# Who issues the three small transfers of the row maxima in a four-layer attention and feed-forward kernel

## The chip, the cores and the metric

The kernel runs on one core of a Trainium2 chip. Its time is the device time of one execution in microseconds (us), inputs and outputs in device memory. Before the change the median of three runs is 6420.63 us, from 6415.23 to 6424.23.

## The reference

Sixteen sequences (B = 16) of 512 tokens of width 256 go through four residual layers, each after a layer norm. The second input is a context of 1601 tokens for each sequence.

```
x = x + attention0(norm(x), ctx)      # 16 heads of 16; q and k are layer-normed per head, scores times 4, softmax, then Wp
x = x + ffn0(norm(x))                 # 256 -> 64 -> 1024, gelu, -> 64 -> 256
x = x + attention1(norm(x), ctx)      # one head of 16, scores normalised over a row, softmax, head tiled 16 times, Wout
x = x + soft_moe(norm(x))             # logits with phi, softmax over the batch and over slots, 64 experts of 256 x 256
```

What matters here is layer 0: for each sequence and each of 16 heads a 512 x 1601 matrix of scores, its row maxima, its exponentials, and their product with the values.

## The kernel before, in words

The kernel has two stages. `stage_one` (to about 4400 us of the profile) computes the first three layers, `stage_two` the last one. The change is in `stage_one` alone.

**Groups and steps.** The 16 heads of a sequence ("image" `b`) are taken in G = 4 groups of HG = 4 heads. There are 64 groups in all, numbered n = 4b + g. The 1601 keys are cut into KC = 13 chunks, of which the last has 65 keys. One step is one key chunk of one group, so a group has 13 steps (c = 0 to 12) and an image has 52. In a step TensorE computes four transposed score tiles, one a head (`score_columns`, matmul at L832), ScalarE takes the exponential of each (`exponentials`, L1107, `probs`), and TensorE multiplies them with the values (`weigh_values`, L843).

**Row maxima.** The softmax needs each query's maximum. It is computed one group ahead: TensorE computes the scores of group n + 1 in 64 pieces (`row_piece`, L810), VectorE reduces them (L1271). In step c = 11 of group n the negated maxima are transposed, and VectorE splits them into three bf16 parts (`maxima_rows`, L1285 to L1289), 16 rows of 128 in the tile `nT`, and raises `nm_ready`. Three transfers of 4 KB then write the parts into rows 96 to 98 of the query stack `qst` of group n + 1 (`load_maxima`, L592, semaphore `nm_loaded`), so that the score matmul, which contracts over 99 rows, subtracts the maximum by itself. Hence the first score matmul of a group waits for the transfers:

```
if c == 0 and j == 0:
    pe.wait_ge(nm_loaded, 48 * (b * G + g + 1))
```

**What else is woven in.** All other work of stage one is cut into small operations. The table `WOVEN` gives each a place: a step and one of three places in it. Every engine walks through steps and places in the same order and does its own part of each operation. This work belongs to other images: the head of image b + 1 (projections, norms, the bf16 planes of its keys and queries) and the tail of image b - 1 (output projection, the two later layers).

**Queues.** In stage one every transfer is issued by SyncE, in the order of that walk: blocks of the context (`ld`, tile `cin`), planes and values stored and loaded again (`ldS`: twelve loads into `kst` and `qst` for one group; `ldV`: `vaug`), the tail's `xw` and `kv1T` (`ldX`), and its stores (`st3`). SyncE issues the maxima of group n + 1 at the start of step c = 12 of group n, ahead of that step's woven work. ScalarE issues no transfer in stage one; in stage two it issues the stores of `logit_scratch`, `y_scratch` and `out`.

Of the kernel before, what the change touches and what calls it, by code (L numbers as in the profile page):

```python
# [12 lines left out]
P = 128  # L13
B, S, D = 16, 512, 256
NK = 1601
QT = S // P
KC = -(-NK // P)
# [3 lines left out]
G = H // HG  # L21
# [17 lines left out]
def key_rows(c):  # L39
    return P if c < KC - 1 else KL  # L40
# [196 lines left out]
OUT_STEP, MAX_STEP = 2, KC - AHEAD  # L237
# [83 lines left out]
def stage_one(nc, x, ctx_d, mask, w, x3_d, xn_d, xnT_d, ident, psum):  # L321

    with ExitStack() as st:
# [48 lines left out]
        qst = [sb(f"qst{g}", [P, HG, S], BF16) for g in range(G)]  # L372
# [4 lines left out]
        nT = sb("nT", [HG * QT, 3, P], BF16)  # L377
# [52 lines left out]
        nm_ready = sem("nm_ready")  # L430
        nm_loaded = sem("nm_loaded")
# [25 lines left out]
        def woven_steps(it, steps, s, place):  # L457

            for of, label in WOVEN[s][place]:
                b = it + of  # L460
                if 0 <= b < B and label[0] in steps:
                    steps[label[0]](b, *label[1:])

        def alone(it, steps):
            for s in range(STEPS):
                for place in range(3):
                    woven_steps(it, steps, s, place)
# [4 lines left out]
        def _(sp):  # L472
# [113 lines left out]
                sp.wait_ge(t_act, at("t_act", b, "xT", 3, 1))  # L586
                sp.dma_start(xnT_d[b], xnT[:, :, :]).then_inc(x_stored, 16)

            def load_maxima(n):
                sp.wait_ge(nm_ready, n + 1)  # L590
                for r in range(3):
                    sp.dma_start(qst[n % G][96 + r:97 + r, :, :].rearrange("o j (t q) -> o (j t) q", q=P),  # L592
                                 nT[:, r, :]).then_inc(nm_loaded, 16)

            steps = {"ld": load_block, "stV": store_values, "stkv1": store_keys_one, "stX": store_planes,
                     "ldS": load_stacks, "ldV": load_values, "ldX": load_tail, "st3": store_tail}

# [1 line left out]
            sp.wait_ge(setup_pool, SETUP_POOL)  # L599
            alone(-2, steps)  # L600
            alone(-1, steps)
            load_maxima(0)
            for b in range(B):
                for s in range(STEPS):
                    n, c = b * G + s // KC, s % KC
                    if c == MAX_STEP + 1 and n + 1 < B * G:
                        load_maxima(n + 1)
                    for place in range(3):
                        woven_steps(b, steps, s, place)
            alone(B, steps)  # L610
# [433 lines left out]
        def _(act):  # L1044
# [57 lines left out]
            def exponentials(b, g, c, j):  # L1102
                m, k = key_rows(c), STEPS * b + KC * g + c
                act.wait_ge(s_full, 4 * k + j + 1)
                if j == 0 and k >= 2:
                    act.wait_ge(pv_mm, k - 1)
                fn(probs[0:m, 4 * (k % 2) + j, :], bank[S_BANK[j % 2]][0:m, :], ACT.Exp,  # L1107
                   scale=float(HD) ** 0.5).then_inc(s_exp, 1)

            def heads_copied(n):  # L1110
                act.wait_ge(pv_mm, KC * (n + 1))
                if n >= 1:
                    act.wait_ge(m_full, RING["out", n - 1] + 1)
                fn(o_sb[:, :], bank[V_BANK], ACT.Copy).then_inc(o_copied, 1)
# [49 lines left out]
                     "s1": layer_one_exp, "o1": layer_one_copied}  # L1164

            alone(-1, steps)
            for b in range(B):
                for s in range(STEPS):
                    g, c = s // KC, s % KC
                    n = b * G + g  # L1170
                    exponentials(b, g, c, 0)
                    if c == 1 and n >= 1:
                        heads_copied(n - 1)
                    woven_steps(b, steps, s, 0)
                    exponentials(b, g, c, 1)
                    woven_steps(b, steps, s, 1)
                    exponentials(b, g, c, 2)
                    woven_steps(b, steps, s, 2)
                    exponentials(b, g, c, 3)
            heads_copied(B * G - 1)  # L1180
            alone(B, steps)

# [705 lines left out]
```

## Time and profile before

| | before |
|---|---|
| median of three runs | 6420.63 us |
| profiled execution | 6438.05 us |
| its span, first to last instruction | 6436.0 us |
| TensorE busy | 5770.0 us, 90% |
| VectorE busy | 3625.0 us, 56% |
| ScalarE busy | 3263.2 us, 51% |
| GpSimd busy | 2413.9 us, 38% |
| mean granted clock of TensorE | 0.955 |

The profile is of one execution. In it PE is TensorE (PEld its weight loads), DVE VectorE, ACT ScalarE, POOL GpSimd, SP SyncE; a `q` behind the name (SPq, ACTq) marks what the engine's queue of instructions does itself, such as issuing a transfer. "L832" is line 832 of the kernel. A tile's name stands as `output<-inputs`. A busy TensorE is not TensorE at its peak, since matmuls are pipelined and their ends are modelled. The granted clock is the share of full speed, 2.4 GHz, that TensorE was given; 0.5 is 1.2 GHz. In the timelines times count from the first instruction; neighbouring instructions of one line are merged into one row with their count ("x3"), and a row that is the first of an answer may start with the first instruction that still ran in the window asked for.

### The profile page before, as it was taken

The page shows a single profiled execution, that of the slowest core. Times are in us where ns is not written, and L with a number is a line of the kernel's source. Part 1 is how long each engine was busy: PE and PEld are TensorE (multiplying, and loading weights), DVE is VectorE, ACT ScalarE, POOL GpSimd, SP SyncE. Part 2 cuts the span into 40 slices and gives each one's busy share as a digit, 9 for nine tenths or more (in the row PEclk, how much of TensorE's full clock was granted, in tenths as well). Part 3 has the DMA queues.
Part 4 walks back from the last instruction along what each step waited for, and adds up shares of the span by engine and source line. Part 5 has one row for each costly group of instructions (what it writes and reads, how often), then busy time and mean ns, then how long its engine had stood idle before and what let it go on. Part 6 is the DMA issues. An engine that isn't in the chain of part 4 may idle for free. (4 is left out here: it accounts for less than half of the span.)

```text
span 6436.0 us, 94456 instructions
## 1 busy us (share of the span) xinstructions
PE 5770.0 (90%) x36221; PEld 2996.8 (47%) x36221; DVE 3625.0 (56%) x7015; ACT 3263.2 (51%) x6257; POOL 2413.9 (38%) x2686
## 2 busy tenths in 40 slices
PE   3799999999999998999989999896599999998999
PEld 1223333333333332333323333232488888877888
DVE  3565656656666665665666656660466666652333
ACT  1366666666665666666666666663222222223331
POOL 3226356263462644626436355344122222220000
PEclk9799999999999999999999999997799999999999
DMA  2441432414324233242332432310366666666553
GB/s 57 86 86 50 78 70 63 85 51 77 70 68 83 54 77 66 70 82 60 68 67 71 79 68 65 64 23 16 135 220 214 213 215 210 208 219 243 205 196 118
DMA packets 436274, 683.75 MB, mean 106 GB/s; under 512 B 63376, under 2 KB 336928, under 8 KB 433520
## 3 DMA queue, kind: packets, MB, share of 16 engines
q1 hardware_dynamic: 326000, 568.64, 34.4%
q10 hardware_dynamic: 109824, 109.07, 5.0%
q8 instruction: 288, 4.72, 0.3%
q14 instruction: 162, 1.33, 0.1%
HBM read 458.39 MB, written 218.39 MB: 105 GB/s over the span
## 5 line engine op out<-in xcount | busy, mean ns | idle before, releaser
L1271 DVE TENSOR_REDUCE mx<-psum 128x1 f32<-128x401 f32 x4096 | 2166.8, 569 | 1570.2 <-PE psum L810 1565.1
L1107 ACT ACTIVATE probs<-psum 128x512 f32<-128x512 f32 (+1 forms) x3328 | 1894.1, 601 | 907.9 <-PE psum L832 900.9
L810 PE MATMUL psum<-kst,qst 96*128 96x401 bf16 x4096 | 1365.1, 348 | 86.0 <-DMA qst<-q_planes 35.9
L832 PE MATMUL psum<-qst,kst 99*128 99x512 bf16 (+1 forms) x3328 | 1302.1, 392 | 109.7 <-ACT probs L1107 58.7
L810 PEld LDWEIGHTS psum<-kst,qst 96*128 96x128 bf16 x4096 | 406.3, 99 | 1339.5 <-DVE mx L1271 900.5
L843 PE MATMUL psum<-probs,vaug 128*17 128x512 f32 x6656 | 903.0, 615 | 0.0
L1565 POOL TENSOR_TENSOR disp<-disp,rz 128x2048 f32<-128x2048 f32 x64 | 294.4, 4601 | 930.3 <-DVE rz L1795 930.3
L832 PEld LDWEIGHTS psum<-qst,kst 99*128 99x128 bf16 (+1 forms) x3328 | 335.0, 101 | 522.7 <-ACT probs L1107 262.9
L1584 PE MATMUL psum<-phi,xT 128*128 128x128 f32 x4096 | 514.3, 280 | 39.6 <-DMA xT<-xnT_scratch 33.6
L1599 PE MATMUL psum<-disp,xnb 128*128 128x128 f32 x4096 | 492.7, 279 | 52.9 <-DMA xnb<-xn_scratch 34.2
L1584 PEld LDWEIGHTS psum<-phi,xT 128*128 128x128 f32 x4096 | 482.6, 194 | 87.3 <-issue 80.9
L1599 PEld LDWEIGHTS psum<-disp,xnb 128*128 128x128 f32 x4096 | 476.7, 194 | 62.0 <-DMA xnb<-xn_scratch 36.2
L679 POOL TENSOR_SCALAR rs<-mv 128x4 f32<-128x4 f32 x48 | 11.2, 232 | 1176.9 <-DVE mv L1323 1175.7
L763 PE MATMUL psum<-wkv,cT 128*128 128x512 f32 (+1 forms) x832 | 410.5, 616 | 16.9 <-ACT sq L1074 7.4
L1828 DVE COPY disp<-psum 128x512 f32<-128x512 f32 x256 | 177.0, 692 | 368.2 <-PE psum L1641 368.1
L1653 PE MATMUL psum<-disp 128*128 128x256 f32 x1536 | 367.4, 381 | 5.2 <-DVE xnb L1845 2.5
L1674 ACT ACTIVATE disp<-psum 128x512 f32<-128x512 f32 x256 | 152.2, 597 | 432.1 <-PE psum L1584 432.0
L1700 ACT ACTIVATE xT<-xT,nm 128x512 f32<-128x512 f32 x256 | 181.0, 709 | 348.2 <-DMA xT<-logit_scratch 339.9
L1802 DVE TENSOR_TENSOR ysb<-psum,be 128x512 f32<-128x512 f32 x128 | 88.6, 692 | 461.0 <-PE psum L1614 450.4
L1706 ACT ACTIVATE slT<-psum 128x512 f32<-128x512 f32 x128 | 76.4, 597 | 435.9 <-PE psum L1599 435.9
L1653 PEld LDWEIGHTS psum<-disp 128*128 128x128 f32 x1536 | 276.4, 190 | 40.4 <-DVE xnb L1845 5.6
L1614 PE MATMUL psum<-we,slT 128*32 128x256 f32 x4096 | 247.7, 382 | 0.0
(198 smaller groups left out, 7467.5 us busy)
## 6 DMA issues: line engine op xcount, KB each, us to landing
xnb<-xn_scratch SPq DMA_DIRECT2D x256, 512.0 KB, 3.7
kst<-k_planes SPq DMA_DIRECT2D x384, 200.1 KB, 8.8
logit_scratch<-disp ACTq DMA_DIRECT2D x64, 1024.0 KB, 4.9
xT<-logit_scratch SPq DMA_DIRECT2D x32, 2048.0 KB, 7.9
k_planes<-pl SPq DMA_DIRECT2D x96, 384.0 KB, 3.2
y_scratch<-ysb ACTq DMA_DIRECT2D x128, 256.0 KB, 4.9
vaug<-v_scratch SPq DMA_DIRECT2D x64, 442.0 KB, 3.7
v_scratch<-vst SPq DMA_DIRECT2D x48, 544.0 KB, 3.1
```

What stands on the lines that cost most here:

```text
L763: last = mm(hb[0:m, :], cT[:, n % 2, k, a * P:a * P + m], wkv[:, k, :], start=(k == 0), stop=(k == 1))
L810: mm(to[:, 0:PW], qst[g][0:NP, j, t * P:(t + 1) * P], kst[g][0:NP, j, k0:k0 + PW], start=True, stop=True).then_inc(m_full, 1)
L832: mm(bank[S_BANK[n % 2]][0:m, :], kst[g][0:NR, j, c * P:c * P + m], qst[g][0:NR, j, :], start=True, stop=True).then_inc(s_full, 1)
L843: last = mm(bank[V_BANK][32 * j:32 * j + HV, :], vaug[0:m, g % 2, c, HV * j:HV * (j + 1)], probs[0:m, 4 * (k % 2) + j, :], start=(c == 0), ...
L1107: fn(probs[0:m, 4 * (k % 2) + j, :], bank[S_BANK[j % 2]][0:m, :], ACT.Exp, scale=float(HD) ** 0.5).then_inc(s_exp, 1)
L1271: v.tensor_reduce(mx[:, n % 2, u // 4, u % 4:u % 4 + 1], bank[HOMES[r][0]][:, 0:PW], AX.X, ALU.max).then_inc(m_free, 1)
L1565: pool.tensor_tensor(d, d, rz[:, n % 2, None, :].broadcast_to((P, B, SL)), ALU.mult).then_inc(normed, 1)
L1584: last = mm(bank[u % 4][:, a * SL:(a + 1) * SL], xT[:, 4 * q + a, k, t * P:(t + 1) * P], phi[:, k, s * SL:(s + 1) * SL], start=(k == 0), s ...
L1599: last = mm(bank[4 + n % 2][:, (2 * a + h) * SL:(2 * a + h + 1) * SL], xnb[:, a, t, h * P:(h + 1) * P], disp[:, (QT * s + t) % RING, b, :] ...
L1614: last = mm(bank[6 + n % 2][32 * j:32 * j + 32, a * D:(a + 1) * D], slT[:, n % 2, a, k, 32 * j:32 * j + 32], we[:, s % 2, j, k, :], start= ...
L1653: last = mm(bank[4 + t][:, a * D:(a + 1) * D], exT[n % 4][:, t * P:(t + 1) * P], ya[b % 4][:, e, :], start=(e == 0 and a == 0), stop=(e == ...
L1700: fn(d, d, ACT.Exp, bias=nm[:, t, b:b + 1], accum_out=sums[:, b % 4, t, h:h + 1]).then_inc(c_exp, 1)
```

## The change

The three transfers of `load_maxima` are taken out of SyncE's program and put into ScalarE's, one behind each of the exponentials 0, 1 and 2 of step c = 12, so ahead of that place's woven work. The first of them waits for `nm_ready`. For the first group of all, ScalarE issues the three together before the first step. What is transferred, the semaphores and every other place stay as they are.

```
--- before.py
+++ after.py
@@ -586,12 +586,6 @@
                 sp.wait_ge(t_act, at("t_act", b, "xT", 3, 1))
                 sp.dma_start(xnT_d[b], xnT[:, :, :]).then_inc(x_stored, 16)
 
-            def load_maxima(n):
-                sp.wait_ge(nm_ready, n + 1)
-                for r in range(3):
-                    sp.dma_start(qst[n % G][96 + r:97 + r, :, :].rearrange("o j (t q) -> o (j t) q", q=P),
-                                 nT[:, r, :]).then_inc(nm_loaded, 16)
-
             steps = {"ld": load_block, "stV": store_values, "stkv1": store_keys_one, "stX": store_planes,
                      "ldS": load_stacks, "ldV": load_values, "ldX": load_tail, "st3": store_tail}
 
@@ -599,12 +593,8 @@
             sp.wait_ge(setup_pool, SETUP_POOL)
             alone(-2, steps)
             alone(-1, steps)
-            load_maxima(0)
             for b in range(B):
                 for s in range(STEPS):
-                    n, c = b * G + s // KC, s % KC
-                    if c == MAX_STEP + 1 and n + 1 < B * G:
-                        load_maxima(n + 1)
                     for place in range(3):
                         woven_steps(b, steps, s, place)
             alone(B, steps)
@@ -1107,6 +1097,12 @@
                 fn(probs[0:m, 4 * (k % 2) + j, :], bank[S_BANK[j % 2]][0:m, :], ACT.Exp,
                    scale=float(HD) ** 0.5).then_inc(s_exp, 1)
 
+            def load_maxima(n, r):
+                if r == 0:
+                    act.wait_ge(nm_ready, n + 1)
+                act.dma_start(qst[n % G][96 + r:97 + r, :, :].rearrange("o j (t q) -> o (j t) q", q=P),
+                              nT[:, r, :]).then_inc(nm_loaded, 16)
+
             def heads_copied(n):
                 act.wait_ge(pv_mm, KC * (n + 1))
                 if n >= 1:
@@ -1164,17 +1160,27 @@
                      "s1": layer_one_exp, "o1": layer_one_copied}
 
             alone(-1, steps)
+            for r in range(3):
+                load_maxima(0, r)
             for b in range(B):
                 for s in range(STEPS):
                     g, c = s // KC, s % KC
                     n = b * G + g
+
+                    def maximum_row(r):
+                        if c == MAX_STEP + 1 and n + 1 < B * G:
+                            load_maxima(n + 1, r)
+
                     exponentials(b, g, c, 0)
+                    maximum_row(0)
                     if c == 1 and n >= 1:
                         heads_copied(n - 1)
                     woven_steps(b, steps, s, 0)
                     exponentials(b, g, c, 1)
+                    maximum_row(1)
                     woven_steps(b, steps, s, 1)
                     exponentials(b, g, c, 2)
+                    maximum_row(2)
                     woven_steps(b, steps, s, 2)
                     exponentials(b, g, c, 3)
             heads_copied(B * G - 1)
```

## Rows read from the trace of the kernel before

**Rows 1.** Waits by engine: us in all, times, longest; TensorE, 236 to 4400 us.

```profile
PE psum L832 <- DMA qst<-nT: 46.6, 12, 5.7
```

**Rows 2.** The view of the tile nT: issues, and landing times.

```profile
L592 SPq DMA_DIRECT2D qst<-nT x192: 502/589/1610, 241.4 to 4344.4; - x192
...
DMA to landing us min/median/max: 1.6/2.1/11.9
```

**Rows 3.** Timeline (start, length, what) of SyncE's queue at a third change.

```profile
3299.20 2.68 SPq L557 DMA_DIRECT2D kst<-k_planes  x6
...
3316.37 1.84 SPq L592 DMA_DIRECT2D qst<-nT  x3
3323.20 2.65 SPq L557 DMA_DIRECT2D kst<-k_planes  x6
```

**Rows 4.** Timeline of TensorE: among them the first and last of 12 waits.

```profile
417.95 0.61 PE L832 MATMUL psum<-qst,kst 99*128 99x512 bf16 x1 [5.68 <-DMA qst<-nT]
...
3322.78 0.38 PE L832 MATMUL psum<-qst,kst 99*65 99x512 bf16 x1
...
3329.59 0.61 PE L832 MATMUL psum<-qst,kst 99*128 99x512 bf16 x1 [5.16 <-DMA qst<-nT]
...
4124.74 0.61 PE L832 MATMUL psum<-qst,kst 99*128 99x512 bf16 x1 [4.43 <-DMA qst<-nT]
```

**Rows 5.** Windows: length, PE, PEld, DVE, ACT, POOL busy, PE clock, DMA, GB/s.

```profile
3329.00:3332.00 3.00, 2.41 (x6) 0.94 (x8) 1.15 (x2) 1.20 (x2) 0.00 (x0) 0.50 1.07 132
```

**Rows 6.** Timeline of SyncE's queue at an image change.

```profile
1260.92 1.77 SPq L592 DMA_DIRECT2D qst<-nT  x3
1263.05 0.39 SPq L572 DMA_DIRECT2D xw<-in_x  x1
...
1264.03 0.47 SPq L579 DMA_DIRECT2D kv1T<-kv_scratch  x1
```

**Rows 7.** Timelines of ScalarE and TensorE at that image change.

```profile
1263.93 1.08 ACT L1107 ACTIVATE probs<-psum 65x512 f32<-65x512 f32 x2
...
1265.47 0.38 PE L832 MATMUL psum<-qst,kst 99*128 99x512 bf16 x1
```

**Rows 8.** Timeline of ScalarE in stage two: issues of its own.

```profile
4707.02 2.31 ACTq L1712 DMA_DIRECT2D y_scratch<-ysb  x1
...
4733.57 0.60 ACT L1674 ACTIVATE disp<-psum 128x512 f32<-128x512 f32 x1 [1.19 <-PE psum L1584]
4733.58 0.37 ACTq L1712 DMA_DIRECT2D y_scratch<-ysb  x1
```

**Rows 9.** Timeline of ScalarE at a first and a second change.

```profile
1332.44 1.08 ACT L1107 ACTIVATE probs<-psum 65x512 f32<-65x512 f32 x2
...
1674.48 0.59 ACT L1107 ACTIVATE probs<-psum 65x512 f32<-65x512 f32 x1
```

**Rows 10.** Timeline of TensorE at the same two changes.

```profile
1335.02 0.38 PE L832 MATMUL psum<-qst,kst 99*128 99x512 bf16 x1
...
1677.81 0.38 PE L832 MATMUL psum<-qst,kst 99*128 99x512 bf16 x1
```

**Rows 11.** Timelines at third changes, without a wait and with one.

```profile
1736.59 2.24 ACT L1107 ACTIVATE probs<-psum 65x512 f32<-65x512 f32 x4
...
1737.33 0.38 PE L832 MATMUL psum<-qst,kst 99*128 99x512 bf16 x1
...
3323.53 1.07 ACT L1107 ACTIVATE probs<-psum 65x512 f32<-65x512 f32 x2
```

**Rows 12.** Transfers issued in 4729 to 4735, then in 4750 to 4757 us.

```profile
y_scratch<-ysb ACTq DMA_DIRECT2D x1, 256.0 KB, 2.9
...
y_scratch<-ysb ACTq DMA_DIRECT2D x1, 256.0 KB, 5.6
```

**Rows 13.** Timeline of SyncE's queue just before the second of those stretches.

```profile
4748.77 0.43 SPq L1494 DMA_DIRECT2D we<-in_L_ffn_W  x1
```

**Rows 14.** Transfers issued in 1264 to 1265 us: size, us to landing.

```profile
kv1T<-kv_scratch SPq DMA_DIRECT2D x1, 8.1 KB, 3.9
```

More of the change, by code:

```diff
@@ L587, in store_tail @@
                 sp.dma_start(xnT_d[b], xnT[:, :, :]).then_inc(x_stored, 16)
[L589 to L593, printed above, removed]
             steps = {"ld": load_block, "stV": store_values, "stkv1": store_keys_one, "stX": store_planes,
@@ L601, in _ @@
             alone(-1, steps)
-            load_maxima(0)
             for b in range(B):
                 for s in range(STEPS):
-                    n, c = b * G + s // KC, s % KC
-                    if c == MAX_STEP + 1 and n + 1 < B * G:
-                        load_maxima(n + 1)
                     for place in range(3):
@@ L1108, in exponentials, with load_maxima @@
                    scale=float(HD) ** 0.5).then_inc(s_exp, 1)
+            def load_maxima(n, r):
+                if r == 0:
+                    act.wait_ge(nm_ready, n + 1)
+                act.dma_start(qst[n % G][96 + r:97 + r, :, :].rearrange("o j (t q) -> o (j t) q", q=P),
+                              nT[:, r, :]).then_inc(nm_loaded, 16)
             def heads_copied(n):
@@ L1166, in _ @@
             alone(-1, steps)
+            for r in range(3):
+                load_maxima(0, r)
             for b in range(B):
@@ L1170, in _, with maximum_row @@
                     n = b * G + g
+                    def maximum_row(r):
+                        if c == MAX_STEP + 1 and n + 1 < B * G:
+                            load_maxima(n + 1, r)
                     exponentials(b, g, c, 0)
+                    maximum_row(0)
                     if c == 1 and n >= 1:
@@ L1175, in _ @@
                     exponentials(b, g, c, 1)
+                    maximum_row(1)
                     woven_steps(b, steps, s, 1)
                     exponentials(b, g, c, 2)
+                    maximum_row(2)
                     woven_steps(b, steps, s, 2)
```

## The prediction

> **What bounds the kernel now.** I read the page's busy shares first, then the waits of TensorE, the view of the tile `nT`, and last the timelines around the places where one group of heads gives way to the next. TensorE is busy for 90% of the span (the table above). It takes its instructions in the order written, so in the first stage (to about 4400 us) a wait of TensorE is time added to the end unless a later wait shrinks by it. One wait there belongs to this change: TensorE stands before the first score matmul of a group (L832) for the maxima rows, 12 times, 46.6 us together, 5.7 us the longest [rows 1]. The wait does not come from a late issue: SyncE issues the three transfers about when `nT` is ready, spending 0.59 us on each, but they land after 1.6 us at best, 2.1 us as the median and 11.9 us at worst [rows 2].
>
> The slow landings have one place. An image has four groups, so 64 groups have 63 changes between them. I call the change from group 0 to 1 "first", 1 to 2 "second", 2 to 3 "third", and into group 0 of the next image "image change". The timeline of TensorE has all 12 waits at third changes, from the one of image 0, ended at 417.95, to that of image 14, ended at 4124.74 [rows 4]. The one of image 11: SyncE has put the stacks of later groups into its queue from 3299.20 on; the maxima are issued at 3316.37 into the same queue, behind that backlog, and the score matmul starts at 3329.59 after 5.16 us of waiting [rows 3, 4]. Afterwards the matmul takes 0.61 us where one before took 0.38, and the granted clock of 3329 to 3332 is 0.50, which is 1.2 of 2.4 GHz, after TensorE had stood still [rows 4, 5]. So a long wait costs more than its length. I estimate 1.2 us more each (one stretch of some 3 us at half speed does half its work, less what TensorE would have waited anyway). Before: 46.6 + 12 x 1.2 = 61 us that the change can win at most.
>
> **The change, part by part.**
>
> *Removed from SyncE*: 192 issues of 0.59 us [rows 2] and its wait for `nm_ready`. Worth nothing: SyncE's next operations wait for their own data (at an image change `xw` goes out at 1263.05, after the maxima's issue is over [rows 6]), and no TensorE wait but the one above is for a late issue of SyncE's. Were it wrong, loads would go out up to 3 x 0.59 = 1.8 us earlier, which could add to the traffic that the maxima meet.
>
> *Added to ScalarE*: the same 192 issues. The wait for `nm_ready` is free: at the image change the maxima were ready when SyncE issued them at 1260.92, and the last key chunk's exponentials that ScalarE must first reach run around 1263 to 1264 [rows 6, 7]. What is queued behind it, the exponentials and all woven copies, therefore does not stand. The issue itself: ScalarE's issue of `y_scratch` starts 0.01 us after an activation of 0.60 us and takes 0.37 us, within it [rows 8], so an issue hides under the exponential ahead of it. For these small transfers I take SyncE's 0.59 us against exponentials spaced 0.5 to 0.6 us: 0 to 0.2 us of delay a group. The dear end is an issue of 2.31 us, right behind a 1 MB store on the same queue [rows 8]. I take nothing for the delay in itself and keep 1 us x 15 image changes in the range.
>
> *Moved in time*: this is the cost. Before, all three were out when `nT` was ready, some 4.5 us ahead of the score matmul at an image change (1260.92 against 1265.47 [rows 6, 7]). After, the third goes out no sooner than the third exponential of the last chunk has begun. How long that is before the score matmul, read off the timelines without a wait:
> - first change: 1332.44 starts a row of two exponentials, the second of them is ours, at 1332.9; matmul 1335.02: 2.1 us [rows 9, 10].
> - second change: 1674.48 against 1677.81: 3.3 us [rows 9, 10].
> - third change: 1736.59 against 1737.33: 0.7 us [rows 11].
> - image change: 1263.93 against 1265.47: 1.5 us [rows 7].
>
> A transfer alone lands in about 1.7 us (between the 1.6 and the 2.1 of rows 2). So first and second changes stay free, while third and image changes wait **always**: at least 1.0 us and 0.2 us.
>
> *Third changes (15 of 16 with loads about)*: the backlog of SyncE's queue is now in another queue than the maxima. From below: the transfer runs as if alone, 1.7 - 0.7 = 1.0 us. From above: it still goes behind everything, and in image 11 behind a `kst` load issued at 3323.20, just ahead of our 3323.55 [rows 3, 11]; then it lands about when it does now or a little later, near 4.4 us. Nearest to it is ScalarE's `y_scratch` under SyncE's loads: 2.9 us in a usual stretch, 5.6 us in a stretch ahead of which, at 4748.77, SyncE had issued a 1 MB load [rows 12, 13], so a tax of up to 2.7 us behind a big load, and here the loads just ahead are small (200 KB) and the big backlog was given out 13 us ago. I take a tax of 0.8 us: 1.8 us x 15 = 27, and 1.0 for the last image, together 28 us.
>
> *Image changes (15)*: about our third issue (1263.93 plus some 0.2, so 1264.1) SyncE has just issued `xw` of 512 KB at 1263.05 and the `kv1T` loads to 1264.03 [rows 6]. From below, alone: 1264.1 + 1.7 = 1265.8, 0.4 us late. From above: like the 8.1 KB `kv1T` transfer that goes out at 1264.03 behind the same loads and takes 3.9 us [rows 6, 14]: 1267.9, 2.5 us late. The y_scratch pair says that a load issued just before on the other queue does hold a transfer up; I take 2.2 us, x 15 = 33 us.
>
> *Aftermath of the waits*: 30 waits near or above 1 us instead of 12 long ones; shorter ones should slow the clock less often, so 0.8 us each, 24 us; first and second changes 2 us in all.
>
> Sum after: 28 + 33 + 24 + 2 = 87 us, against 61 us before: **26 us slower**. The profiled execution took 6438.05 us (span 6436.0), which makes 6464; it lies 17 us above the median of the runs, so on the median's scale 6420.6 + 26 = 6447 us.
>
> The Trainium skill has a rule that speaks about the same disputed point. Its page "DMA: Bandwidth & Descriptors", section "Queues, rings and completion order", says that each of the DMA engines takes turns between the queues by packets of typically 9 to 17 descriptors, so a small transfer on a second queue would wait for one packet at most, not for a backlog. The 5.6 us against 2.9 us of rows 12 does not look like that; by the rule the image change would be near its low end and the result the first rival's.
>
> **Rivals.**
>
> *Faster: the second queue passes everything.* If the maxima wait for no more than the few descriptors under way, third changes cost 1.4 x 15 + 1 = 22 us, image changes 0.6 x 15 = 9, aftermath 10, together 41 against 61: 20 us faster, 6401. The place is ScalarE's empty queue in the first stage, the price what is left of the landing after the third exponential; it decides if the tax at an image change stays under about 1 us. For it: nothing else is on that queue before 4400 us. Against: rows 12.
>
> *Even.* The taxes come out between, say 1.4 us at image changes and 1.6 at third ones: 21 + 25 + 18 = 64 against 61, within 13 us of 6421.
>
> *Much slower: the backlog holds the second queue too.* Third changes 4.4 x 15 = 66 us, image changes 2.5 x 15 = 38, aftermath 30 x 0.8 = 24: 128 against 61, 67 slower, 6488. It decides from the point where the maxima land with the `kst` load issued before them. For it: rows 12. Against: the backlog at a third change was issued long ago, in small pieces.
>
> That the change does nothing is excluded by the order written: the third issue stands behind an exponential that begins 0.7 us before the matmul.
>
> **How the numbers follow.** Forecast 0.45, faster rival 0.22, even 0.2, much slower 0.13. The forecast's own range is 6430 to 6465. A measurement of this kernel can tell about 0.2%, 13 us, from no change (its three runs span 9 us). Faster by more: 0.2; within: 0.26, with edges of the forecast and the faster rival; slower: 0.54. The range for 8 in 10 reaches 22 us down and 61 up: 6398 to 6482.
>
> **What would show it.** Right: the wait for `qst<-nT` appears some 30 times, of 1 to 3 us, none above 3.5; it is at every image change, where there was none, and at every third change; none at second changes; the landing of the transfers has a median near 2 us and a worst of 4 to 5 us; ScalarE's busy time is the same. Wrong: landings at image changes under 2.2 us (the tax is not there, the faster rival), or waits of 4 us and more at third changes (the backlog holds both queues), or a first change that waits, or exponentials that stand behind issues of over 1 us. If the waits come out as said and the time does not, the term for the clock is at fault.

## The result, and the profile after

| | before | after |
|---|---|---|
| median | 6422.43 us (4 runs) | 6533.5 us (4 runs, 6508.97 to 6544.69) |
| profiled execution / its span | 6438.05 / 6436.0 us | 6528.45 / 6526.7 us |
| ratio after to before | | 1.0166, 95% interval 1.0132 to 1.0200 |
| first score matmul of stage one to the last | 4149.5 us | 4237.7 us |
| waits of TensorE for the maxima | 47 us | 99 us |
| time lost to the lower clock in stage one | 124 us | 159 us |

The change makes the kernel 111 us slower on the medians, 90 us between the two profiled executions. Of these, 88 us lie in stage one. The last row sums (1 - granted clock) over the clock records between the first and the last score matmul: 3.4 us at half clock lose 1.7. The two sums grow by 52 and by 35 us, 87 together, so the 88 us are accounted for. The other 20 us between 111 and 90 are the place of the profiled executions among the runs: the one before lies 16 us above its median, the one after 5 us below.

The waits of TensorE in stage one of the kernel after (against [rows 1]), and the view of `nT` (against [rows 2]); `L822` is the score matmul's line now, `L1103` that of the transfers:

```profile
PE psum L822 <- DMA qst<-nT: 99.3, 44, 5.3
PE psum L867 <- POOL xn L672: 67.9, 30, 2.9
PE psum L822 <- ACT probs L1097: 55.1, 90, 1.8
```

```profile
L1103 ACTq DMA_DIRECT2D qst<-nT x192: 510/527/1336, 237.7 to 4435.0; - x192
...
DMA to landing us min/median/max: 1.6/2.4/7.5
```

12 waits have become 44 (the view leaves out waits of under 0.15 us). The worst landing has come down from 11.9 to 7.5 us, but only because the transfers start later. Summed by place, the waits are: third changes 40.6 us (15 and one of 0.1 us; before 47.0 with the last image's), image changes 52.0 us (15, before 0.1), second changes 6.2 us (1.7 in image 0, 0.1 to 0.5 in 13 others), the very first group 0.7.

The image change into image 4 (against [rows 6] and [rows 7]), on the timelines of SyncE's queue, of ScalarE and of TensorE:

```profile
1273.97 0.38 SPq L572 DMA_DIRECT2D xw<-in_x  x1
1274.45 0.59 SPq L577 DMA_DIRECT2D kv1T<-kv_scratch  x1
1275.08 0.70 SPq L579 DMA_DIRECT2D kv1T<-kv_scratch  x1
```

```profile
1273.78 0.59 ACT L1097 ACTIVATE probs<-psum 65x512 f32<-65x512 f32 x1 [0.88 <-PE psum L822]
1273.78 0.57 ACTq L1103 DMA_DIRECT2D qst<-nT  x1
1274.40 0.59 ACT L1097 ACTIVATE probs<-psum 65x512 f32<-65x512 f32 x1
1274.42 0.57 ACTq L1103 DMA_DIRECT2D qst<-nT  x1
1275.04 0.59 ACT L1097 ACTIVATE probs<-psum 65x512 f32<-65x512 f32 x1
1275.06 0.58 ACTq L1103 DMA_DIRECT2D qst<-nT  x1
```

```profile
1280.63 0.61 PE L822 MATMUL psum<-qst,kst 99*128 99x512 bf16 x1 [3.92 <-DMA qst<-nT]
```

The reader sees each issue start with an exponential and end under it: ScalarE as an issuer costs nothing to speak of. The first transfer goes out at 1273.78, 0.2 us ahead of `xw`; the other two go out behind it. What that does to their landings, of the three, and what the neighbours took (transfers issued in 1273 to 1277):

```profile
DMA to landing us min/median/max: 1.7/4.5/5.5
```

```profile
xw<-in_x SPq DMA_DIRECT2D x1, 512.0 KB, 4.7
...
qst<-nT ACTq DMA_DIRECT2D x3, 4.0 KB, 4.5
kv1T<-kv_scratch SPq DMA_DIRECT2D x2, 8.1 KB, 5.4
```

1.7 us for the one ahead, 4.5 and 5.5 us for those behind. The third, 4 KB out of ScalarE's empty queue, takes as long as the two 8.1 KB `kv1T` transfers of SyncE's (5.4 us is the middle of 4.8 and 6.0), which were given out behind the same load.

Third changes show the same more plainly, since the backlog there is old. ScalarE and TensorE at that of image 11, where the first transfer was issued at 3386.91:

```profile
3388.42 0.51 ACTq L1103 DMA_DIRECT2D qst<-nT  x1
...
3390.14 0.51 ACTq L1103 DMA_DIRECT2D qst<-nT  x1
3390.28 0.68 ACT L1151 ACTIVATE hx<-psum,maskb 128x512 f32<-128x512 f32 x1
3390.85 1.07 ACT L1097 ACTIVATE probs<-psum 65x512 f32<-65x512 f32 x2
```

```profile
3395.91 0.39 PE L822 MATMUL psum<-qst,kst 99*128 99x512 bf16 x1 [4.17 <-DMA qst<-nT]
```

The last row of ScalarE holds the exponentials 2 and 3. The third issue, written behind exponential 2, went out 0.71 us before that exponential began, while ScalarE was still at two woven activations; so it is at 14 of the 16 third changes (0.87 us at the last one, not at the first). The packets by queue, first in 3387 to 3391.4, then in 3391.4 to 3393.4 (q1 is SyncE's queue, q10 ScalarE's):

```profile
q1 hardware_dynamic: 469, 0.55, 106.8%
```

```profile
q1 hardware_dynamic: 189, 0.30, 106.7%
q10 hardware_dynamic: 90, 0.01, 8.8%
```

For 4.5 us after the first issue not one packet of ScalarE's queue moves, while the stacks that SyncE had given out ahead of the transfers (24 loads for two groups, issued from 3366.43 to 3377.7 here, as the ones from 3299.20 on in [rows 3]) are worked off; then 90 packets of it move within 2 us. The order is not strict: when the first of them moved, five of the 24 loads had still to land, and the last of these landed at 3394.84, between the second transfer (3394.61) and the third (3395.87). Over all third and image changes of the kernel after, 373 of 392 times a transfer of SyncE's that had been issued earlier and was still out landed before the one of the maxima, the other 19 times at most 0.9 us behind it; of 564 issued later, while one of the maxima was still out, 546 landed behind it.

The clock behind the image change, the windows 1281 to 1285 and 1285 to 1289 of the kernel after, where the kernel before had 1.00 at the same place (columns as in [rows 5]):

```profile
1281.00:1285.00 4.00, 4.00 (x17) 3.06 (x16) 1.95 (x5) 2.28 (x4) 0.20 (x1) 0.50 1.08 137
1285.00:1289.00 4.00, 4.00 (x15) 0.73 (x13) 1.25 (x3) 1.64 (x3) 4.00 (x1) 0.50 1.03 127
```

### The profile page after: what moved, and what is told of

It reads as the page before. It is cut to its first block and busy times, and to the rows that moved or that the text cites. A ratio compares the mean times of both kernels' runs of the same rounds, so it can differ in the third digit from the quotient of the medians.

```text
span 6526.7 us, 94456 instructions
## 1 busy us (share of the span) xinstructions
PE 5805.8 (89%) x36221; PEld 3010.5 (46%) x36221; DVE 3629.4 (56%) x7015; ACT 3268.7 (50%) x6257; POOL 2408.9 (37%) x2686
## 5 line engine op out<-in xcount | busy, mean ns | idle before, releaser
L822 PE MATMUL psum<-qst,kst 99*128 99x512 bf16 (+1 forms) x3328 | 1314.4, 395 | 160.8 <-DMA qst<-nT 99.3
L822 PEld LDWEIGHTS psum<-qst,kst 99*128 99x128 bf16 (+1 forms) x3328 | 336.6, 101 | 586.8 <-ACT probs L1097 267.0
```

What stands on the lines that cost most here:

```text
L822: mm(bank[S_BANK[n % 2]][0:m, :], kst[g][0:NR, j, c * P:c * P + m], qst[g][0:NR, j, :], start=True, stop=True).then_inc(s_full, 1)
```

## The experiments

All ratios are to the kernel before, measured on the same chip, with 95% intervals; 3 rounds each. "Waits" are those of TensorE for the maxima, "clock" the time lost as in the table above, both of the profiled execution. The kernel before was run again with each set of kernels, with medians of 6414.52 to 6423.13 us by chip; a ratio is to the one of its own set.

| kernel | median us | ratio | waits us | clock us |
|---|---|---|---|---|
| before | 6423.13 (25 runs) | | 47 | 124 |
| after | 6533.5 | 1.0166 [1.0132, 1.0200] | 99 | 159 |
| act_early | 6427.61 | 0.9997 [0.9984, 1.0010] | 42 | 120 |
| sp_late | 6426.47 | 1.0005 [0.9992, 1.0018] | 47 | 108 |
| tail_after | 6454.85 | 1.0043 [1.0028, 1.0057] | 48 | 101 |
| stack_later | 6348.82 | 0.9881 [0.9863, 0.9898] | 0 | 75 |
| xw_rows | 6531.43 | 1.0172 [1.0148, 1.0197] | 88 | 147 |
| filled | 6536.83 | 1.0194 [1.0165, 1.0223] | 70 | 148 |
| stack_after | 6527.1 | 1.0167 [1.0132, 1.0201] | 94 | 147 |
| before_filled | 6407.94 | 0.9978 [0.9963, 0.9994] | 32 | 87 |
| paced | 6554.76 | 1.0208 [1.0181, 1.0235] | 93 | 165 |
| stack_paced | 6652.21 | 1.0366 [1.0346, 1.0387] | 187 | 236 |
| sp_behind | 6544.77 | 1.0200 [1.0168, 1.0233] | 129 | 188 |
| filled_long | 6487.34 | 1.0127 [1.0098, 1.0155] | 30 | 85 |

**act_early: the issuer alone.** From the changed kernel, `maximum_row` taking the step as well; each `+` names the call that now stands behind that exponential:

```
 exponentials(b, g, c, 0);  + maximum_row(MAX_STEP + 1, 2)      # maximum_row(at_c, r): if c == at_c
 exponentials(b, g, c, 2);  + maximum_row(MAX_STEP, 0)
 exponentials(b, g, c, 3);  + maximum_row(MAX_STEP, 1)
```

> The changed kernel, but ScalarE issues the three transfers as soon as the maxima are ready: behind exponentials 2 and 3 of step 11 and exponential 0 of step 12, about when SyncE issued them before. Theory A (what costs is the late issue, by which the transfers fall behind the loads that SyncE issues around an image change; queue and issuing engine matter little, and a transfer keeps its turn behind everything issued earlier on either queue): no waits for the maxima at image changes and second changes, third changes wait as in the kernel before (2 to 5 us each, 40 to 50 us in all), time 6410 to 6440 us. Theory B (ScalarE as issuer costs by itself, by blocking its queue): time stays above 6480 us. Theory C (a queue of its own lets the transfers pass the backlog if they are out early): third changes wait under 1 us each, time 6360 to 6390 us.

The time is that of the kernel before. ScalarE as issuer costs nothing measurable (B falls), and a queue of its own gives nothing (C falls): early out on the empty queue, the transfers still took up to 10.5 us at third changes.

```profile
PE psum L822 <- DMA qst<-nT: 42.1, 15, 6.0
```

**sp_late: the lateness alone.** From the kernel before:

```
+ sp.wait_ge(s_full, 4 * (KC * n - 1) + r + 1)      # before issue r, at place r of step 12
```

> The kernel before, with SyncE as issuer, but each of the three issues waits until the score tile of exponential 0, 1 and 2 of step 12 is there, so they go out as late as in the changed kernel, yet in SyncE's own order, ahead of the loads of the next image change. Theory A (being late costs by what it falls behind; no queue is special): image changes wait 0.2 to 0.6 us each, third changes 2 to 5 us as in the changed kernel, the sum of waits 50 to 60 us, time 6420 to 6450 us. Theory D (being late by itself costs what was seen, loads ahead or not): image changes wait about 3.4 us each, time 6500 us or more.

The same late issues on SyncE's queue, where `xw` comes behind them by the order written, cost nothing measurable. Image changes wait 0.20 us in most images (5.4 us in all), third changes 42 us. So lateness is not the price; what is let in front is. (The sum of the waits, 47 us, is a little under the 50 to 60 expected.)

**sp_behind: one queue, loads in front.** sp_late, with the loads of `xw` and `kv1T` moved between the first and the second transfer:

```
-    put(0.0, -1, "ldX")
+    put(51.0, 0, "ldX")
```

> sp_late (SyncE issues everything, the maxima late), but the loads of xw and kv1T of the image change are issued between the first and the second maxima transfer, about where they fall in time in the changed kernel. Theory A (both queues are served in the order of issue, so whose queue it is makes no difference): image changes wait 3 to 4.5 us each and the time is 6490 to 6560 us. Theory K (a second queue makes it worse than one: the transfers lose their turn to the other queue): waits of 1.5 to 2.5 us on one queue, the time at most 6475 us.

With everything in one queue the loss of the change is back, and the time is in theory A's range (K falls). The image change of image 4 waits 5.23 us:

```profile
1288.53 0.61 PE L835 MATMUL psum<-qst,kst 99*128 99x512 bf16 x1 [5.23 <-DMA qst<-nT]
```

The waits are longer than theory A said (88 us over 15 image changes, 5.9 each), because the second and third issue also queue behind five issues of 0.5 us on SyncE: the third goes out 1.3 us after TensorE began to wait, where it went out 1.6 us ahead of that in the kernel after. The landings themselves are no longer: the third took 4.5 us in the mean of the 15 image changes, against 5.0 in the kernel after.

**tail_after: two queues, loads held back.** From the changed kernel:

```
 sp.wait_ge(x_stored, at("x_stored", b - 1, "st3"))
+if b + 1 < B:
+    sp.wait_ge(nm_loaded, 48 * (G * (b + 1) + 1))
 sp.dma_start(xw...)
```

> The changed kernel, but at an image change SyncE holds back the loads of xw and kv1T until the three transfers have landed. Theory A (the wait at image changes comes from these loads, issued on the other queue just ahead of the second and third transfer): the wait there falls from 3.4 to 0.2 to 0.7 us each, the landing of the third transfer from 5.2 to about 2 us, time falls by 60 to 90 us to 6440 to 6470 us. Theory E (ScalarE's queue itself is slow to land what it issues back to back): the waits stay near 3 us and the time above 6500 us.

The waits at image changes fall from 52.0 us to 4.3, most of them 0.10 us each; at the one around 1263 us all three land in 1.7 us:

```profile
DMA to landing us min/median/max: 1.7/1.7/1.7
```

79 us of the 111 come back by this one wait of SyncE, and what remains is within 32 us of the kernel before. E falls. (Its runs spread from 6423 to 6462 us, and the profiled one is the lowest of ten, so the sums in the table flatter it.)

**paced: SyncE held back as before, but not issuing.** From the changed kernel, at the start of step 12:

```
+ sp.wait_ge(nm_ready, n + 2)
```

> The changed kernel, but SyncE still waits for nm_ready at the start of step 12, as it did when it issued the maxima, and issues nothing there. Theory A: nothing is queued behind that point that matters (the loads of the image change and of the third change come at the same times), so waits and time stay as in the changed kernel, 6515 to 6545 us. Rival J (part of the loss is that SyncE is no longer held back and its loads crowd the transfers): time falls by 20 us or more.

No gain (J falls); the time is 10 us above the range of theory A, and the ratio if anything a little above that of the kernel after (the intervals overlap).

**xw_rows: as many bytes, a quarter of the pieces.** From the changed kernel:

```
-sp.dma_start(xw[:, :, :], x[b].rearrange("(t p) d -> p t d", p=P))
+sp.dma_start(xw[:, :, :], x[b].rearrange("(p t) d -> p t d", p=P))
```

> The changed kernel, but the load of xw at an image change (512 KB) is read in 128 pieces of 4 KB instead of 512 pieces of 1 KB; the same bytes, other token order, so what the layers behind it compute is another permutation of the tokens. Theory A1 (the transfers wait for the bytes ahead of them to pass): waits at image changes stay at 3 to 3.5 us, time 6515 to 6540 us. Theory A2 (they wait for the pieces ahead to be made and taken one by one): the wait falls by 0.7 to 1.5 us each, time by 15 to 45 us.

This kernel is for its time alone: its tokens come into `xw` in another order than what is added to them, so its output is another. In the trace the load moves in 128 packets of 4 KB. Waits at image changes go from 3.5 to 3.1 us, the time stays (A1): the number of pieces of this load is not what the transfers wait for, in the main.

**stack_later: the backlog out of the way of the kernel before.**

```
-    put(head["X", 4, 0] + 2.2, 1, "ldS", 1)
+    put(39.2, 1, "ldS", 1)
```

> The kernel before, with one edit of the table: the twelve loads of group 1's stacks of the next image move from step 33.7 to 39.2, behind the third change. Theory A (the waits of the kernel before at third changes come from the backlog of these loads alone): the 12 waits vanish (under 5 us in all), landings of the maxima are at most 3 us, and with less time at half clock the kernel takes 6360 to 6385 us, faster than both. Rival F (the backlog moves with the loads and something else waits: the values, the context block or the first scores of the next image's groups): a new wait of similar size, time within 0.3% of 6422 us.

The waits are gone: in the waits of TensorE no row names `nT` any more, and the view of the tile has

```profile
DMA to landing us min/median/max: 1.6/1.7/3.6
```

It is 1.19% faster than the kernel before and the best of all. At 6348.8 it lies 11 us below A's range, so the gain was larger than expected: in the profile the lower clock costs 75 us in place of 124, so 50 us less. What share of the miss that is, no run tells. F falls.

**stack_after and stack_paced: the same edit on the changed kernel.** stack_after is the `put` above on the kernel after; stack_paced adds the wait of paced.

> The changed kernel with the loads of group 1's stacks moved behind the third change (as in stack_later), to see what the change costs where no backlog is. Theory A: third changes wait 0.9 to 1.3 us each (only the late issue), image changes 3 to 3.5 us each as before, first changes none; sum of waits 65 to 75 us and with the clock the kernel is 75 to 105 us slower than stack_later, 6425 to 6455 us. Rival (with the backlog gone the second queue is free and the loads of the image change no longer matter): within 30 us of stack_later, under 6380 us.

> stack_after with the same wait of SyncE for nm_ready kept, so that the moved loads of group 1's stacks can't run ahead of the third change. Theory A: third changes wait 0.9 to 1.4 us each (16 us in all, only the late issue), image changes 3 to 3.6 us each (50 us), second changes 0.3 to 0.5; with the clock 85 to 125 us slower than stack_later, 6435 to 6475 us. Rival (the second queue is taxed by any traffic): third changes stay above 2.5 us and the time above 6500 us.

Both expectations missed. In stack_after the waits at third changes remained at 38 us. SyncE's timeline shows why: the loads of group 1's stacks (the second pair of rows) went out at once behind those of group 0, ahead of the transfers (from 1212.31 on), although the table puts them behind the third change.

```profile
1192.27 2.68 SPq L557 DMA_DIRECT2D kst<-k_planes  x6
1194.99 2.77 SPq L559 DMA_DIRECT2D qst<-q_planes  x6
1197.81 2.77 SPq L557 DMA_DIRECT2D kst<-k_planes  x6
1200.62 2.77 SPq L559 DMA_DIRECT2D qst<-q_planes  x6
```

SyncE runs ahead of the steps as far as its waits let it. What held it at the third change in stack_later was its own wait for `nm_ready`, which the change had moved to ScalarE. With that wait back (stack_paced) it issues the twelve loads the moment the maxima are ready, at 1231.36, while ScalarE issues them from 1234.58 to 1237.81, and TensorE waits longest of all:

```profile
1231.36 2.65 SPq L557 DMA_DIRECT2D kst<-k_planes  x6
1234.05 2.78 SPq L559 DMA_DIRECT2D qst<-q_planes  x6
```

```profile
1248.59 0.61 PE L825 MATMUL psum<-qst,kst 99*128 99x512 bf16 x1 [9.17 <-DMA qst<-nT]
```

So with the change's issue on ScalarE the kernel with this line moved is 2.8% (stack_after, 6527.1) and 4.8% (stack_paced, 6652.2) slower than without it (6348.8). That is again the order of issue over both queues, here at its dearest.

**filled, before_filled, filled_long: is it the clock?** Extra score matmuls into a bank that is overwritten next, ahead of the wait:

```
+for _ in range(k):      # filled: k = 6 at groups 0 and 3; before_filled: 6 at group 3; filled_long: 16 at group 0, 12 at group 3
+    mm(bank[S_BANK[0]][0:m, :], kst[g][0:NP, 0, 0:m], qst[g][0:NP, 0, :], start=True, stop=True)
 pe.wait_ge(nm_loaded, ...)
```

The wait for the exponentials stands ahead of them now.

> The changed kernel, but at image changes and third changes TensorE runs six extra score matmuls of 0.38 us (into the bank that the next one overwrites) before it waits for the maxima, so it is busy for 2.3 us of a wait of about 3. Theory G (a third of the loss is the half clock after TensorE stood still): the waits shrink by what the fillers take, the time at half clock in the first stage falls from 159 us lost to 100 to 130 us lost, and the time falls to 6480 to 6510 us though no transfer lands earlier. Rival H (the half clock has nothing to do with these waits): lost time by the clock stays near 159 us, time 6530 us or a little above.

> The kernel before with six extra score matmuls ahead of the wait at third changes only. Theory G: the waits shrink from 47 us to about 20 us and the time lost by the clock from 124 to 90 to 110 us; time 6390 to 6415 us. Rival H: time 6423 us or up to 10 us above, since three of the third changes had no wait to fill.

> The changed kernel with 16 extra score matmuls (3.4 us at 0.21 us each) ahead of the wait at an image change and 12 (2.6 us) at a third change, so TensorE hardly stands still in these waits. Theory G (half clock follows standing still): time lost by the clock in the first stage falls from 159 to 90 to 115 us, the waits from 99 to 40 us or less, the time to 6475 to 6510 us. Rival H (the half clock does not follow these waits): lost time by the clock stays above 140 us, time 6530 us or above.

filled settles nothing: in a row the matmuls take 0.21 us each, not the 0.38 that I had reckoned with, so six covered 1.3 us of waits of 3; clock and time hardly moved, and its expectation missed. before_filled gained 0.22% [0.06, 0.37] with 37 us less lost to the clock, though 32 us of waits were left where 20 were expected. filled_long covers the waits. Landings are no earlier, yet the kernel is 46 us faster than the kernel after (6487 against 6533, and 46 us between the profiled executions too), with the clock's loss at 85 us instead of 159. But each was measured against a set of runs of the kernel before of its own; by these ratios, 1.0127 and 1.0166, the gain is 25 us, and their intervals overlap. So a quarter to two fifths of what the change cost is clock (G), as far as these runs tell. That the gain is less than 74 us fits fillers that overrun the shorter waits; that is not shown.

## Why the prediction was wrong

- *Right*: slower; ScalarE's issues hide under exponentials and the wait for `nm_ready` is free; first changes stay free (none waits); image changes and third changes now wait, 3.5 and 2.7 us each in the mean, for the transfer issued third, which lands last. At image changes the third issue is out 1.6 us before TensorE begins to wait, where 1.5 had been read from the timelines. One of the signs named for being wrong came: waits of 4 us and more at third changes (5.3, 4.2 and 4.1 us).
- *The step that failed: the tax on ScalarE's queue*, in both of its places. At third changes I had put the backlog "in another queue than the maxima" and taken a tax of 0.8 us for it, on top of 1.0 us for being late: 28 us foretold, 40.6 measured. The third transfer landed there after 4.2 us in the mean (1.7 to 7.0), not after 1.7 and 0.8, so the tax is 2.5 us. At image changes I took 2.2 us of delay, 33 us foretold, 52.0 measured: the landing took 5.0 us in the mean. Even the upper end of 2.5 us was too low: it was `kv1T`'s landing of 3.9 us in the kernel before, while behind the transfers' new neighbours the same load took 4.8 and 6.0. act_early, sp_late, sp_behind and tail_after show what stands in place of the tax: here a small transfer waits for what was issued earlier, on either queue.
- *A second step, hidden by the first*: "the third goes out no sooner than the third exponential of the last chunk has begun" is not so. At third changes it went out 0.7 us before that, 1.6 us ahead of TensorE's wait and not 0.7. So the 1.0 us for being late was 0.1, and the shortfall of the tax is larger than the sums show. For the same reason the argument that "the change does nothing" is excluded did not hold; the waits at third changes come from the backlog, but for that 0.1 us.
- *Second changes*: 2 us foretold for first and second ones together, 6.2 measured. The context block, which SyncE had issued 3.7 us ahead of the matmul, goes out 0.4 us ahead of the third transfer (at the one of image 11), which lands after 3.8 us; I had looked at the distance to the matmul alone.
- *The aftermath*: 24 against 14 us foretold, so 10 more; 35 more measured. The price of 1.2 us for a long wait was too low already in the kernel before: the stretches at half clock that begin at its 12 waits lose 46 us, 3.8 each. At 14 image changes of the kernel after they lose 61 us, where the kernel before has none. Together the waits grew by 53 us where 16 were foretold, and the clock's loss by 35 where 10 were; that makes 87 or 88 us in the profiles in place of 26.
- *Removed from SyncE, "worth nothing"*: right for the change as made (paced), wrong as a reason: stack_after shows that the wait for `nm_ready` was what kept later loads behind.
- *The rivals*: the mechanism was that of "much slower", to which I gave 0.13. Its waits, 104 us, came out at 99 in all, but by luck: 66 for 40.6 at third changes, 38 for 52.0 at image changes. Its price of 6488 us was 45 us short, mainly 25 by the clock and 20 by the place of the profiled executions among the runs. The two rows of [rows 12] had spoken for it. The rule of the Trainium skill (page "DMA: Bandwidth & Descriptors", section "Queues, rings and completion order"), turns between queues packet by packet, did not tell how long a small transfer waits in stage one, with 4.5 us and 469 packets of one queue before the first of the other. Once they moved, packets of both queues moved in the same 2 us, as turns would have it; whether the transfers came late to these turns, no run shows. The same page's section "Issuing engines are not separate DMA queues" says that issuing from several engines saves only the issuer's time, and act_early agrees that nothing else is won: 0.9997.

## What to carry to other kernels

A second issuing queue is no fast lane: before moving a small urgent transfer to another engine, write down what will have been issued before it on **all** queues, and reorder the bulk loads instead. Here one moved line of the table (stack_later) gave 1.2% where moving the transfers lost 1.7%. A wait in a queue's program is also a fence for everything behind it, so when it goes, ask what now runs ahead; and price a wait of TensorE of about 3 us at more than its length (at image changes here 3.5 us of waiting and 4.1 us to the clock).

## What the runs showed of the hardware that I had not expected

- In stage one the transfers of SyncE's and ScalarE's queues landed nearly in the order in which they were issued, over both (373 of 392, the rest within 0.9 us): 4.5 and 5.5 us for 4 KB behind a 512 KB load on the other queue, 1.7 us with that load held back. Where in the path the order is kept, the runs don't tell; a quarter of the pieces for the same bytes changed the wait by 0.4 us only.
- An issue on ScalarE can go out before the activation that stands ahead of it begins: 0.71 us before it at 14 of 16 third changes, while ScalarE was at other activations.
- At 14 of the 15 image changes of the kernel after, TensorE's wait was followed by 3.4 to 13.7 us at the granted clock 0.50 (not where it had waited 1.9 us); why some are followed by 3.4 us and others by four times that stays open. In the kernel before shorter waits were followed by it too: at 558 us 3.4 us at 0.50 begin 1.8 us behind a wait of 1.15 us.
- Six score matmuls in a row take 1.3 us, not six times the 0.38 us that the profile gives for one, since the modelled durations overlap.
